# Second attention's scores: three passes of 110, 96 and 96 rows against two of 128 and one of 46

## The reference

```python
    def _L1_xattn_ref(x, context, Wq, Wk, Wv, Wo, bo, gamma, beta):
        ...
        h = _layernorm(x, gamma, beta)
        Q = (h @ Wq).reshape(B, NQ, N_HEADS, HEAD_DIM)
        K = (context @ Wk).reshape(B, NC, N_HEADS, HEAD_DIM)
        V = (context @ Wv).reshape(B, NC, N_HEADS, HEAD_DIM)
        attn = jnp.einsum('bihd,bjhd->bhij', Q, K)
        attn = jax.nn.softmax(attn, axis=-1) * scale
        vals = jnp.einsum('bhij,bjhd->bihd', attn, V).reshape(B, NQ, INNER)
        return x + vals @ Wo + bo
```

## Time and profile before

| | us |
|---|---|
| median of 3 runs | 1109.26 (1107.14 to 1110.64) |
| the profiled execution, its own time | 1106.37 |
| its span, first to last instruction | 1104.6 |
| TensorE busy in it | 1026.3 (93%) |
| VectorE, ScalarE, GpSimd busy | 748.1, 571.4, 389.8 |

### The profile page before, as it was taken

The page is one execution under the profiler, slowest core; times in us unless marked ns, Lnnn a source line. Parts: engine busy times, 40 slices in busy tenths (PEclk is TensorE's granted clock), DMA queues, the critical chain, the costliest instruction groups (busy, mean ns, idle before and its releaser), DMA issues. The chain is left out here.

```text
span 1104.6 us, 31648 instructions
## 1 busy us (share of the span) xinstructions
PE 1026.3 (93%) x12060; PEld 742.5 (67%) x12060; DVE 748.1 (68%) x1409; ACT 571.4 (52%) x1139; POOL 389.8 (35%) x273
## 2 busy tenths in 40 slices
PE   5977899999999999979688999999999999999997
PEld 2552577777777776646325777777777778777786
DVE  4657788887888778321794776777676767767752
ACT  2533577777777776631444544445444444544442
POOL 4821121111211123030105554545455454646542
PEclk9988899999999999989798999999999999999998
DMA  3501544444444443030002111111111111012100
GB/s 105 144 2 70 145 133 135 126 152 140 128 132 139 141 123 91 2 99 1 0 23 76 56 56 38 55 38 39 54 56 54 41 49 51 28 52 56 35 4 4
DMA packets 48461, 79.41 MB, mean 72 GB/s; under 512 B 8802, under 2 KB 35252, under 8 KB 48404
## 3 DMA queue, kind: packets, MB, share of 16 engines
q1 hardware_dynamic: 48404, 78.61, 23.8%
HBM read 51.13 MB, written 21.96 MB: 66 GB/s over the span
## 5 line engine op out<-in xcount | busy, mean ns | idle before, releaser
L1376 ACT ACTIVATE P<-PS 125x448 f32<-125x448 f32 x384 | 207.1, 544 | 270.3 <-PE PS L1285 268.4
L1266 POOL TENSOR_TENSOR Pl<-P 125x896 f16<-125x896 f32 x128 | 229.9, 1801 | 242.3 <-ACT P L1376 242.3
L1014 DVE TENSOR_REDUCE m<-PS 128x1 f32<-128x500 f32 x336 | 220.8, 675 | 120.1 <-PE PS L1005 118.3
L920 DVE TENSOR_REDUCE m_part<-PS 128x1 f32<-128x500 f32 x336 | 210.5, 673 | 54.8 <-PE PS L822 53.3
L1301 PE MATMUL PS<-cNh,P 125*128 125x97 f16 x1344 | 198.0, 208 | 0.1
L1303 PE MATMUL PS<-cNh,Pl 125*128 125x97 f16 x1344 | 197.4, 207 | 0.0
L1302 PE MATMUL PS<-cNl,P 125*128 125x96 f16 x1344 | 196.8, 206 | 0.0
L898 ACT ACTIVATE Pb<-PS 125x448 f32<-125x448 f32 x384 | 186.0, 547 | 19.5 <-PE PS L797 18.5
L1302 PEld LDWEIGHTS PS<-cNl,P 125*128 125x128 bf16 x1344 | 131.9, 98 | 25.5 <-issue 0.2
L1301 PEld LDWEIGHTS PS<-cNh,P 125*128 125x128 bf16 x1344 | 131.2, 98 | 15.8 <-issue 3.2
L1283 PE MATMUL PS<-Qh,cTh 110*125 110x448 f16 x384 | 139.0, 362 | 1.3 <-DVE Qh L1452 1.3
(11 more groups left out here) (170 smaller groups left out, 1530.0 us busy)
## 6 DMA issues: line engine op xcount, KB each, us to landing
Kst<-k_halves SPq DMA_DIRECT2D x144, 125.0 KB, 2.8
k_halves<-KH SPq DMA_DIRECT2D x16, 750.0 KB, 3.2
cx<-in_ctx SPq DMA_DIRECT2D x16, 562.5 KB
d_cx<-in_ctx SPq DMA_DIRECT2D x16, 562.5 KB
c_halves<-cHi SPq DMA_DIRECT2D x16, 281.2 KB, 2.6
c_halves<-cLo SPq DMA_DIRECT2D x16, 281.2 KB, 3.0
cTh<-c_halves SPq DMA_DIRECT2D x16, 281.2 KB, 3.0
cTl<-c_halves SPq DMA_DIRECT2D x16, 281.2 KB, 3.8
```

The lines of the kernel that those rows point to most:

```text
L920: nc.vector.tensor_reduce(m_part[:, t, part:part + 1], PS[:, 6 + k % 2, 0:SP], AX.X, ALU.max).then_inc(s_reduced, 1)
L1014: nc.vector.tensor_reduce(m21[:, t, part:part + 1], PS[:, S1[k % 2], 0:SP], AX.X, ALU.max).then_inc(n_red, 1)
L1266: nc.gpsimd.tensor_tensor(Pl[:, c % NP], P1[:, c % NP], high, ALU.subtract).then_inc(n_low_p, 1)
L1376: nc.scalar.activation(P1[:, c % NP, half * HALF:(half + 1) * HALF], PS[0:KC, u % 3, 0:HALF], ACT.Exp).then_inc(n_exp, 1)
```

## The change

Scores of the second attention contract over different groupings of the same 302 rows. `kA`/`qA` hold 128 rows (keys high by queries high, and 32 of keys high by queries low), `kB`/`qB` 128 more, and `kC`/`qC` the last 32 with the 14 of the maximum. `kC` and `qC` hold these 46 rows twice, at partitions 0 and 64, so that the third matmul of a half runs in one of two tiles of 64 rows x 128 columns of the array. Chunks go in groups of two (`GC = 2`): the four halves of a group fill four PSUM banks with their first two passes, then the four third matmuls follow (`score_rests`), then the values of the group before. The pieces of the maximum lose their bank 3 to the scores and share banks 7 and 6 with the turned output; a table PLACES says where in a group they stand. VectorE makes the low part of every fourth chunk instead of every third. Loads of a batch are 12 DMAs instead of 4. The maximum is turned to two places, and laid in two instructions of 512 columns. Three weight tiles of the feed-forward stage now share memory with others.

```diff
-        O1, W1, S1 = 4, 6, (3, 7)
+        O1, W1 = 4, (6, 7)
+        S0, S1 = (3, 7), (7, 6)
...
-        LAG = 2
+        GC = 2
+        NG = NC // GC
...
+        PLACES = [(0, 0, 0, 0, 0, 0), (0, 0, 0, 0, 0, 1), (1, 1, 1, 1, 1, 1), (1, 0, 1, 1, 1, 1), (1, 0, 1, 1, 1, 1), (1, 1, 1, 1, 0, 0), (0,) * 6]
...
-        low_on_dve = [c % 3 == 2 for c in range(NC)]
+        low_on_dve = [c % 4 == 3 for c in range(NC)]
...
+                def score(i, par, u):
...
+                    if u == 2 * GC - 1:
                         pe.wait_ge(n_mlaid, n + 1)
-                    wait_for(pe, n_exp, n * 2 * NC + u - 2)
+                    wait_for(pe, n_exp, n * 2 * NC + u - 3)
-                    o = PS[0:KC, u % 3, 0:HALF]
-                    pe.matmul(o, cTh[:, par, at], Qh[:, par, cols], start=True, stop=False)
-                    pe.matmul(o, cTh[0:DC, par, at], Ql[:, par, cols], start=False, stop=False)
-                    pe.matmul(o, cTl[:, par, at], Qh[0:DC, par, cols], start=False, stop=True).then_inc(n_st, 1)
+                    o = PS[0:KC, u % 4, 0:HALF]
+                    pe.matmul(o, kA[:, par, at], qA[:, par, cols], start=True, stop=False)
+                    pe.matmul(o, kB[:, par, at], qB[:, par, cols], start=False, stop=True)
+
+                def score_rests(par, g):
+                    for c in range(GC * g, GC * g + GC):
+                        at = slice(c * KC, (c + 1) * KC)
+                        for half in range(2):
+                            rows_of, cols = slice(64 * half, 64 * half + 32 + MR), slice(64 * half, 64 * half + HALF)
+                            mm = pe.matmul(PS[0:KC, (2 * c + half) % 4, 0:HALF], kC[rows_of, par, at], qC[rows_of, par, cols],
+                                           start=False, stop=True, skip_group_check=True)
+                        mm.then_inc(n_st, 2)
...
+                    for g in range(NG + 1):
+                        if has_1 and g == NG:
+                            turn_maximum(i, par)
+                        if has_b and g < NG:
+                            for j in range(2 * GC):
+                                score(i, par, 2 * GC * g + j)
+                                if has_old and g == 1 and j < 2:
+                                    turn_output(b - 1, j)
+                                if j < 3:
+                                    pieces(g, j)
+                            score_rests(par, g)
+                        pieces(g, 3)
+                        for j in range(GC):
+                            if has_b and g > 0:
+                                values(i, par, GC * (g - 1) + j, tuple(range(QT)))
+                            pieces(g, 4 + j)
+                        if has_b and has_old and par == 0 and g == 1:
                             project(i - 1)
```

More of the change, by code:

```diff
@@ L1013, in reduce_piece1 @@
             t, part = PIECES1[k]
[L1014 removed]
+            nc.vector.tensor_reduce(m21[:, t, part:part + 1], PS[:, banks[k % 2], 0:SP], AX.X, ALU.max).then_inc(n_red, 1)
         Wvo16 = sb_in(late, "Wvo16", [DC, 2, H, D], F16)
@@ L1328, in turn_maximum @@
                     pe.wait_ge(n_mready, n + 1)
-                    if inside(i, par, 0) and inside(i, par, -1):
-                        pe.wait_ge(n_ot, n * 2 - 2)
-                        if par == 0:
-                            pe.wait_ge(n_y, i)
-                    pe.matmul(PS[96:96 + MR, W1, 0:128], mn1[:], ident, start=True, stop=True).then_inc(n_mturned, 1)
+                    for first in (32, 96):
+                        mm = pe.matmul(PS[first:first + MR, W1[0], 0:128], mn1[:], ident, start=True, stop=True)
+                    mm.then_inc(n_mturned, 1)
                 def body(i, par):
@@ new lines, in lay_maximum @@
+                        for first, t in ((32, 0), (96, QT - 4)):
+                            m = nc.vector.tensor_tensor(qC[first:first + MR, slot].rearrange("p (t q) -> p t q", t=4),
+                                                        spread(PS[first:first + MR, W1[0], 0:128], 1, 4),
+                                                        spread(tab[first:first + MR, C_MM + t:C_MM + t + 4], 2, 128), ALU.mult)
+                        m.then_inc(n_mlaid, 1)
+                    for g in range(NG + 1):
+                        pieces = list(itertools.chain(*BESIDE1[g])) if has_b and has_1 else []
+                        if has_b and has_old and g == 1:
+                            split_old(i, par, 0)
+                            split_old(i, par, 1)
+                        if has_b and has_old and par == 0 and g == 2:
@@ L1469, in body @@
                             finish_tile(i - 1)
-                        if has_1 and c == 10:
+                        for k in pieces[:2]:
+                            reduce_piece1(dve, i, par, k, S1)
+                        if has_1 and g == NG:
                             negate_maximum()
-                        if has_1 and c == NC:
+                        if has_b and g >= 2 and g % 2 == 0:
+                            c = GC * g - 1
+                            dve.wait_ge(n_exp, (b * NC + c + 1) * 2)
+                            high = P1[:, c % NP].bitcast(BF16)[:, 1::2]
+                            nc.vector.tensor_tensor(Pl[:, c % NP], P1[:, c % NP], high, ALU.subtract).then_inc(n_low_d, 1)
@@ L1473, in body @@
+                        for k in pieces[2:]:
+                            reduce_piece1(dve, i, par, k, S1)
+                        if has_1 and g == NG:
                             lay_maximum()
```

153 lines of the change are left out of this document (76 added, 77 removed).

## The result

The changed kernel takes 1119.78 us (median of 4 runs, 1118.70 to 1121.01), the kernel before 1109.15 beside it: a ratio of 1.0099, interval 1.0084 to 1.0114. It is slower by 1.0%, three times the 0.3% that a measurement can tell from no change. Its profiled execution took 1121.01, with a span of 1119.1, against 1106.37 and 1104.6.

The account below looks back on a forecast made before the run. TensorE was taken to bound the last stage, so every stall is paid in full. Terms of +1.53 us a batch, times 14, with +0.4, -2.9 and -1.4, gave +17.5, so 1127 us; 8 in 10: 1108 to 1139.

Parts of the forecast that it names:

- tile pairs: Third passes on TensorE: two 64-row tiles side by side cost the time of one, saving 2.28 us a batch.
- switches: TensorE switching to 64-row tiles and back 6 times a batch, 0.25 us each: +1.50 us a batch.
- maximum turned twice: Turn of the maximum made for two places: one more fp32 pass that doesn't overlap, +0.11 us a batch.
- the turn late: Last group with scores: GpSimd's low part holds VectorE's chain of the maximum, so the turn comes late, +1.1 us a batch.
- fifth score: Between the first two groups: the fifth score waits for the bank that the first exponential frees, +0.5 us a batch.
- pieces behind the low part: Group 2: GpSimd's low part of the context holds VectorE's low part, delaying a reduction and a piece, +0.6 us a batch.
- The ends: Ends of the stage: start -2.9 us (between 0 and -4.5), last batch +0.4, very end -1.4.
- the first: Rival: the tiles run one after the other, giving 1153 us; chance 0.07.
- The second: Rival: the chain of the maximum isn't held, 13.5 us less, giving 1113 us; chance 0.12.
- the third: Rival: array and memory are kinder, the switch costing nothing in fp16: 1110 or 1098 us; chance 0.11 of ending under 1106.
- The fourth: Rival: switches cost more (0.35 each) or pieces also wait in other groups, +10, giving 1137 us; chance 0.12.
- the fifth: Rival: the change does nothing to the bound, gain and cost equal, 1106 to 1112.6 us; chance 0.08.

Follow-up runs that it names:

- e1: Changed kernel with both third passes of a chunk in the same 64-row tile, one after the other: 1144.66 us, ratio 1.0323.
- e10: Changed kernel with, in group 0 alone, chunk 0's third passes issued behind its own scores, ahead of chunk 1's: 1115.35 us, ratio 1.0062.
- e4: Changed kernel with the cast of the context and GpSimd's low part of it one group later: 1115.39 us, ratio 1.0063.
- e7: Changed kernel with, in group 5 alone, chunk 10's third passes issued before chunk 11's scores: 1104.69 us, ratio 0.9974.
- e8: Changed kernel with chunk 10's low part on VectorE and chunk 11's on GpSimd, the reverse of before: 1124.62 us, ratio 1.0163.
- e3: Changed kernel with the turn of the maximum moved from ahead of chunk 10's values to behind them: 1115.64 us, ratio 1.0062.
- after_again: The changed kernel itself run once more, nothing altered: 1119.26 us, ratio 1.0113.
- e11: Changed kernel with third passes of groups 0 and 5 issued chunk by chunk and the context's cast one group later: 1095.60 us, ratio 0.9878.
- e2: Changed kernel with third passes over 96 rows, padded with zeros, so the array is never switched: 1128.09 us, ratio 1.0181.

## Why the prediction was right

The direction, the place and the three waits were as put down; the sum was 17.5 us on a profiled execution, which measured 14.6, and the medians differ by 10.6. 1119.8 is 7 us under the 1127 of the forecast, at the near edge of its 1119 to 1133. Step by step, per batch:

| term | predicted | measured | from |
|---|---|---|---|
| tile pairs | -2.28 | -2.24 | e1: 6 x 0.374 |
| switches | +1.50 | +1.41 | 6 x (0.09 + 0.05 + 0.095) |
| maximum turned twice | +0.11 | 0.02 | below |
| the turn late | +1.1 | +1.07 | from the last value to the turn, 1.29 in place of 0.22 |
| fifth score | +0.5 | +0.60 | e10: 0.32 + 0.285 |
| pieces behind the low part | +0.6 | +0.50 | e4: 0.42, and 0.08 that stays |
| sum | +1.53 | +1.36 | beats: 1.25 (17.54 / 14) |

- **The array.** Right in both parts. Of the three prices of the switch the exposed load of 0.05, which I took between 0.01 and 0.075, is what the second pair shows; its place I had wrong, as I put it ahead of the first pair (0.145 in, where 0.09 is measured) and let the second follow 0.19 behind (0.24 is measured). The load rule that I weighed against it, 0.104 (the Trainium skill, TensorE: Matmul & The Clock Gate, section on LDWEIGHTS), would have put a batch 0.32 higher; the trace shows 0.05 here, half of it. That the other half is hidden behind the switch or the first pair is my reading, and no run shows it.
- **The turn for two places** was mis-sized: its four records end as soon as before's two did. From L1373 to the next matmul it is 0.33 (845.50 to 845.83), against 0.31 in the earlier trace rows. The two places are 32 and 96, in different tiles, and overlap.
- **The maximum** was right in its mechanism and size, L1489 at 1.41 in place of L1441's 0.17. e7 shows it by taking GpSimd's instruction out of the way, e8 by giving it to VectorE, e3 by moving the customer. Against e7 the turn is 1.16 late, but against the kernel before only 1.07: there the turn already comes 0.32 behind the last value's start in every other batch (807.56 to 807.88 in the earlier trace rows), where 0.14 is the step without a wait. The prediction had nothing for this. The start of the exponentials decides it: 1.4 us earlier, and nothing is held, if only by 0.04.
- **The pieces** cost 0.84 and 0.16 in the two kinds of batch, where I had 1.0 and 0.4 less something for before. e4 shows that the context's low part is the cause of the 0.84. The 0.16 is the bank that the projection's result leaves, which I had put down at 0.2; the rows under e4 show it, and no experiment removed it.
- **The sum of a batch** is 0.11 us over the beats. Most of this is a term that I put at nothing: from the first pass of a half to the second it is 0.198 us on average before and 0.193 now, 24 times a batch, 0.10 less.
- **The ends.** The first batch takes 31.33 in place of 36.27: -4.9 instead of my -2.9. I had no wait left for the DMA, in place of 3.45; 1.41 is left in this execution, none in after_again. And I had taken over the work at 1.2 GHz. Granted clock of the kernel before, of the changed one, and of the changed one again, 584 to 588 us (the column behind the fifth count; 1.00 is 2.4 GHz, 0.50 is 1.2):

```profile
584.00:588.00 4.00, 0.59 (x2) 0.00 (x0) 0.00 (x0) 0.60 (x2) 1.68 (x1) 0.50 0.45 149
```

```profile
584.00:588.00 4.00, 3.33 (x17) 1.38 (x16) 0.90 (x2) 2.44 (x5) 2.68 (x2) 1.00 0.90 232
```

```profile
584.00:588.00 4.00, 3.73 (x12) 1.75 (x10) 0.00 (x0) 1.85 (x4) 2.47 (x2) 0.50 0.89 210
```

The same kernel ran through its first batch at 2.4 GHz once and at 1.2 GHz in these four us the other time, and the batch then took 32.22. So 0.9 of the 4.9 goes with the clock and is luck. With the low clock, as I had assumed, it is still 4.05 less and not 2.9; where that last 1.1 lies stays open.

From the last turn to the end it is 40.54 for 41.60, -1.1, where the last batch and the end together had -1.0. That agreement is luck too, since after_again takes 39.23, -2.4. The two executions keep the same times to the start of the last projection; then the clock falls at once in the one and over 1 us later in the other, as the first two us of that stretch show, after first and after_again second:

```profile
1110.59:1112.59 2.00, 1.51 (x14) 1.51 (x15) 0.44 (x2) 0.00 (x0) 0.00 (x0) 0.63 0.04 8
```

```profile
1109.34:1111.34 2.00, 1.51 (x27) 1.51 (x28) 0.44 (x2) 0.00 (x0) 0.00 (x0) 0.99 0.04 8
```

- **The profiled pair and the medians.** Steady batches +17.5, first -4.9, end -1.1 make +11.5. The other 3.0 of the spans lie ahead of the stage and are within its scatter (after_again). 11.5 stands well beside the medians' 10.6; with after_again's stage it is 17.5 - 4.05 - 2.4 = 11.1. In either case 21.4 for the fourteen batches was 4 us too much, and -2.9 for the start 1 to 2 us too small a gain.

Of the rivals, e1 rules out the first. The second (a chain that isn't held) and the third (a faster kernel) are not this kernel, but e7 shows the second one placement away, and e11 is faster, though not by the third's mechanism, as its switches cost what they did: the gain of the tile pairs, 0.84 a batch net, is real, and 2.2 us of waits lay on it. The fourth falls with a switch at 0.235, and with pieces that wait in no other group; the fifth with the medians. That no wait for a DMA stands in the list behind the stage's start bears out the larger loads that I put at nothing.

## What to carry to other kernels

Grouping passes to save switches delays whoever reads the group's results: price the engines behind, from the last pass of the group, at the two places where a batch begins and ends, and split the group there. Where VectorE and GpSimd share work, ask which of the two starts first at every meeting, since a short link of a critical chain can be held for nearly the length of the other's longest instruction (1.69 us for 0.17 in the earlier trace rows); in e8 0.02 us lay between the one that kept its time and the one that was held. Two row tiles side by side, with passes of 448 columns as here, are worth their switch only in groups: 0.374 saved for 0.235 in a group of four passes, 0.19 for 0.235 in a pair alone.

## What the runs showed of the hardware

- Two matmuls in tiles of 64 rows, fp16, 448 columns, start 0.003 us apart and take the time of one (e1 against the changed kernel: 0.97 and 0.59 for four).
- In and out of this tiling costs 0.09 and 0.095 us, and 0.05 for a first load of weights that is not hidden. The Trainium skill (TensorEngine Tiling (Array Packing), section Key Properties) says that a change of the tiling mode drains the engine; the trace shows a loss at each change, which fits, and these are its prices here. e2, without the change of mode, has no such loss.
- Held instructions were longer by nearly the rest of the other's: 1.41 for 0.17, 2.10 and 2.44 for 1.08 on VectorE, 2.60 for 1.68 on GpSimd. Reductions of VectorE were not held: L1042 takes 0.66 to 0.68 in the changed kernel, the 143 that start beside a GpSimd instruction and the 169 that don't.
- The granted clock of the stage's first 10 us and of its end differs between executions of the same program; with it the first batch differed by 0.9 us and the end by 1.3.
